# Cross-attention block on one core: score products in four 32-row tiles with unmasked keys, and every round as straight code

## The reference, cut to what matters

```python
def attention(q, k, v, mask):                      # A and B
    scores = jnp.einsum('bhqd,bhkd->bhqk', q, k) / jnp.sqrt(jnp.float32(HD))
    scores = scores * mask - 10000.0 * (1.0 - mask)
    probs = jax.nn.softmax(scores, axis=-1)
    return jnp.einsum('bhqk,bhkd->bhqd', probs, v)
...
scores = jnp.einsum('bhtd,bhsd->bhts', Q, K) * scale     # C
scores = jnp.where(mask, scores, jnp.float32(-jnp.inf))
attn = jax.nn.softmax(scores, axis=-1)
```

## Time and profile before

| what | value |
|---|---|
| median of 3 runs | 1069.2 us (1064.68 to 1073.83) |
| profiled execution, span | 1072.6 us, 3.4 us above the median |
| mean granted TensorE clock | 0.947 of full |
| PE, PEld busy | 967.9 us (90%), 929.0 us (87%) |
| DVE, ACT, POOL busy | 866.5 us (81%), 576.3 us (54%), 561.3 us (52%) |
| instructions | 23111, of them PE 8336 matmuls |
| chain that ended last | PE 44%, DVE 32%, issue 11%, POOL 6%, ACT 6% |
| DMA | 25.74 MB, 24 GB/s on average |

### The profile page before, as it was taken

One profiled execution on the slowest core, in us unless ns is written; L12 is line 12 of the kernel. 1 busy time (PEld: TensorE's weight loads), 2 busy tenths in 40 slices (PEclk: granted clock), 3 DMA queues, 4 the chain that ended last, 5 costly groups with the idle time before them and its releaser, 6 DMA issues.

```text
span 1072.6 us, 23111 instructions
## 1 busy us (share of the span) xinstructions
PE 967.9 (90%) x8336; PEld 929.0 (87%) x8336; DVE 866.5 (81%) x1946; ACT 576.3 (54%) x1109; POOL 561.3 (52%) x566
## 2 busy tenths in 40 slices
PE   6977799999999998999999898999999899998876
PEld 6866798989989998988999898998999899998875
DVE  6586979888897978889797988889797888778553
ACT  3444646565474556646464656547455664646342
POOL 2254647457283746638274745728474563727221
PEclk9589999998999899999989999899989999898995
DMA  5030100101000010101001010100101010000000
GB/s 192 0 96 1 36 1 12 37 11 36 11 10 26 9 35 10 35 10 35 10 0 35 10 35 10 35 10 0 35 10 35 10 36 1 26 13 7 17 10 10
DMA packets 32936, 25.74 MB, mean 24 GB/s; under 512 B 12672, under 2 KB 32000, under 8 KB 32896
## 3 DMA queue, kind: packets, MB, share of 16 engines
q1 hardware_dynamic: 32896, 25.20, 7.9%
HBM read 20.99 MB, written 4.19 MB: 23 GB/s over the span
## 4 chain that ended last, share of the span: by engine, by line
PE 44%; DVE 32%; issue 11%; POOL 6%; ACT 6%; DVEq 1%; DMA 0%; ACTq 0%; POOLq 0%; SPq 0%
PE s_bank L504 12%; PE pj L446 10%; PE s_bank L493 7%; PE pj L431 6%; DVE o L866 5%; PE pj L460 4%; DVE rmax_A L852 3%; POOL prob_AC L1089 2%; DVE prob_AC L847 2%; DVE stats L892 2%; DVE z_A L906 2%; PE pj L521 2%; DVE rmax_C L852 2%; PE s_bank L482 2%; DVE z_B L906 2%
## 5 line engine op out<-in xcount | busy, mean ns | idle before, releaser
L683 ACT ACTIVATE k<-pj,kbias,consts 128x256 f32<-128x256 f32 x192 | 92.7, 564 | 143.1 <-PE pj L431 143.1
L1065 POOL TENSOR_TENSOR veps<-mv,eps 128x2 f32<-128x2 f32 x64 | 15.6, 243 | 263.2 <-DVE mv L898 263.2
L1089 POOL TENSOR_TENSOR prob_AC<-prob_AC,rmax_C 128x512 f32<-128x512 f32 x64 | 65.6, 1054 | 125.4 <-DVE rmax_C L852 125.4
L692 ACT ACTIVATE prob_AC<-prob_AC 128x512 f32<-128x512 f32 x128 | 81.1, 636 | 89.5 <-POOL prob_AC L1089 89.4
L1096 POOL TENSOR_TENSOR h_lo<-g,h_hi 128x512 fp32r<-128x512 f32 x64 | 81.4, 1292 | 47.3 <-DVE h_hi L1051 47.3
L482 PE MATMUL s_bank<-k,q 64*128 64x128 f32 x1536 | 100.3, 281 | 6.3 <-ACT q L670 3.8
L482 PEld LDWEIGHTS s_bank<-k,q 64*128 64x128 f32 x1536 | 91.0, 191 | 14.2 <-issue 4.7
L504 PE MATMUL s_bank<-vz_C,prob_AC 128*128 128x66 f32 x512 | 74.7, 316 | 16.5 <-ACT prob_AC L698 16.5
L504 PEld LDWEIGHTS s_bank<-vz_C,prob_AC 128*128 128x128 f32 x512 | 72.7, 231 | 19.5 <-issue 19.4
L1080 POOL TENSOR_TENSOR prob_AC<-prob_AC,maskA_off 128x512 f32<-128x512 f32 x64 | 79.9, 1284 | 17.2 <-DVE prob_AC L847 17.2
L1080 POOL TENSOR_TENSOR prob_B<-prob_B,maskB_off 128x512 f32<-128x512 f32 x64 | 83.0, 1329 | 10.7 <-DVE prob_B L847 10.6
(11 more groups left out here) (199 smaller groups left out, 3324.7 us busy)
## 6 DMA issues: line engine op xcount, KB each, us to landing
x_in<-in_x SPq DMA_DIRECT2D x16, 256.0 KB, 2.7
ctx_b<-in_ctx SPq DMA_DIRECT2D x16, 256.0 KB, 2.9
ctx_c<-in_ctx SPq DMA_DIRECT2D x16, 256.0 KB, 2.8
out<-y SPq DMA_DIRECT2D x16, 256.0 KB, 2.2
g<-in_w_M SPq DMA_DIRECT2D x2, 1024.0 KB, 7.1
maskB<-in_mask_Bx1xSxS_ff SPq DMA_DIRECT2D x32, 64.0 KB, 2.6
prob_AC<-in_w_A_qkv SPq DMA_DIRECT2D x1, 768.0 KB, 4.5
prob_B<-in_w_B_kv SPq DMA_DIRECT2D x1, 512.0 KB, 6.1
```

What stands on the lines that cost most here:

```text
L683: last = nc.scalar.activation(k2[:, m, :, s, :], k_all[:, m], ACT.Identity, bias=kbias[:, "ABC".index(a), s, m:m + 1], scale=parity[:, 2 + ...
L692: nc.scalar.activation(p2, p2, ACT.Exp).then_inc(exped[a], 1)
L1089: nc.gpsimd.tensor_tensor(p3, p3, rmax[a][:, r, :].unsqueeze(2).broadcast_to([P, BL * TILE, S]), ALU.subtract).then_inc(shifted[a], 1)
```

## The change

The keys are kept once (k1, without the parity scaling or the second copy): two activations, with the plain bias. A score product contracts over 32 partitions, which are one head pair (two heads), and streams 64 columns. There are 32 products for an attention: for each t, c, b2 the four row groups r = 0..3, and row group r writes bank r. All four banks are waited for before the first product and handed over with the last (t, c, b2). A bank now holds one row group for both tiles, so the order of head pairs in prob, sums and o changes, and with it the access patterns of masks, offsets, values and normalisation. The stationary operand q2 is as before. kbias is dropped. `run` has no loop: all rounds are straight code.

```diff
-        k2 = sb("k2", [P, KC, UB, 2, S])
+        k1 = sb("k1", [P, KC, UB, S])
...
-        def of_tile(m, a, r):
-
-            t = r // HALVES
-            m = m[:, :, :] if a == "A" else m[:, t * TILE:(t + 1) * TILE, :]
-            return m.rearrange("p b k -> p (b k)").unsqueeze(1).broadcast_to([P, BL, TILE * S])
+        def by_tile(scores):
+
+            return scores.rearrange("p (t c) k -> p t c k", t=T)
+
+        def of_tiles(m, a):
+
+            if a == "A":
+                m = m.rearrange("p b k -> p (b k)").unsqueeze(1).broadcast_to([P, T, TILE * S])
+            else:
+                m = m.rearrange("p (t b) k -> p t (b k)", t=T)
+            return m.unsqueeze(2).broadcast_to([P, T, KC, TILE * S])
...
-            for i in range(first, min(FIRST, last + 1)):
-                body(i)
-            with eng.Fori(FIRST, U) as i:
-                body(i)
-            for i in range(U, last + 1):
+            for i in range(first, last + 1):
                 body(i)
...
+                wait_score_banks(f"S_{a}", i, R - 1)
                 for t in range(T):
-                    wait_score_banks(f"S_{a}", i, HALVES * (t + 1) - 1)
                     for c in range(KC):
                         for b2 in range(TILE):
-                            for half in range(HALVES):
-                                rows_ = slice(half * S, (half + 1) * S)
-                                bank = s_bank[t * HALVES + half][:, :].rearrange(
-                                    "p (c s b k) -> p c s b k", c=KC, s=2, b=TILE)
-                                mm = nc.tensor.matmul(bank[:, c, :, b2, :],
+                            for r in range(R):
+                                rows_ = slice(r * 2 * HD, (r + 1) * 2 * HD)
+                                at = ((t * KC + c) * TILE + b2) * S
+                                mm = nc.tensor.matmul(s_bank[r][:, at:at + S],
                                                       q2[rows_, c, t * TILE + b2].rearrange("p e q -> p (e q)"),
-                                                      k2[rows_, c, t * TILE + b2], start=True, stop=True)
-                                if (c, b2) == (KC - 1, TILE - 1):
+                                                      k1[rows_, c, t * TILE + b2], start=True, stop=True)
+                                if (t, c, b2) == (T - 1, KC - 1, TILE - 1):
                                     mm.then_inc(scored[a], 1)
...
-                for s in range(2):
-                    for m in range(KC):
-                        last = nc.scalar.activation(k2[:, m, :, s, :], k_all[:, m], ACT.Identity,
-                                                    bias=kbias[:, "ABC".index(a), s, m:m + 1],
-                                                    scale=parity[:, 2 + s:3 + s])
+                for m in range(KC):
+                    last = nc.scalar.activation(k1[:, m, :, :], k_all[:, m], ACT.Identity,
+                                                bias=bias[:, BK[a] + m:BK[a] + m + 1])
...
-                nc.vector.tensor_tensor(prob[a][:, r, :, :], s_bank[r][:, :].rearrange("p (n k) -> p n k", n=BL),
-                                        of_tile(m, a, r), f).then_inc(masked[a], 1)
+                nc.vector.tensor_tensor(by_tile(prob[a][:, r, :, :]),
+                                        s_bank[r][:, :].rearrange("p (t c k) -> p t c k", t=T, c=KC),
+                                        of_tiles(m[:, :, :], a), f).then_inc(masked[a], 1)
...
-                            o[rows_, t * TILE:(t + 1) * TILE, half * BL:(half + 1) * BL, :],
-                            sums[rows_, :, e * HD:(e + 1) * HD].rearrange("p (n b) f -> p b n f", b=TILE),
-                            rden[a][rows_, r, :].rearrange("p (n b) -> p b n", b=TILE).unsqueeze(3).broadcast_to(
-                                [S, TILE, BL, HD]), ALU.mult)
+                            o_r[rows_],
+                            sums[rows_, :, e * HD:(e + 1) * HD].rearrange("p (c b) f -> p c b f", c=KC),
+                            rden[a][rows_, r, :].rearrange("p (c b) -> p c b", c=KC).unsqueeze(3).broadcast_to(
+                                [S, KC, UB, HD]), ALU.mult)
...
-                    p3 = prob[a][:, r, :, :]
-                    nc.gpsimd.tensor_tensor(p3, p3, of_tile(maskA_off if a == "A" else maskB_off, a, r),
-                                            ALU.add).then_inc(offset[a], 1)
+                    p4 = by_tile(prob[a][:, r, :, :])
+                    m = maskA_off if a == "A" else maskB_off
+                    nc.gpsimd.tensor_tensor(p4, p4, of_tiles(m[:, :, :], a), ALU.add).then_inc(offset[a], 1)
```

More of the change, by code:

```diff
@@ L158, in build @@
         qbias = sb("qbias", [P, 2, 2, KC])
-        kbias = sb("kbias", [P, 3, 2, KC])
         brow = sb("brow", [P, 3, H])
@@ L501, in values @@
                 pe.wait_ge(turned_in[a], R * u + r + 1)
-                t, half = divmod(r, HALVES)
+                half, s = divmod(r, 2)
                 for n in range(BL):
-                    last = nc.tensor.matmul(s_bank[r][:, n * TILE * VW:(n + 1) * TILE * VW],
-                                            prob[a][:, r, n, :], vz[a][:, t, half * BL + n, :, :],
+                    t, c = divmod(n, KC)
+                    at = c * T + t
+                    last = nc.tensor.matmul(s_bank[r][:, at * TILE * VW:(at + 1) * TILE * VW],
+                                            prob[a][:, r, n, :], vz[a][:, t, half * BL + c * 2 + s, :, :],
                                             start=True, stop=True)
@@ L809, in finish_biases @@
                     if stage != "C":
[L810 to L814, removed]
+                        last = nc.vector.tensor_scalar(qbias[:, "AB".index(stage), e, :],
+                                                       bias[:, BQ[stage]:BQ[stage] + KC],
+                                                       qscale[:, e:e + 1], None, ALU.mult)
+                        if e == 1:
+                            last.then_inc(bias_done, 1)
+                    elif e == 1:
+                        nc.vector.nop().then_inc(bias_done, 1)
             def low_part(name, i, bias_cols=None):
@@ L858, in normalise @@
                     dve.wait_ge(summed[a], R * u + r + 1)
-                    t, half = divmod(r, HALVES)
+                    half, s = divmod(r, 2)
                     sums = s_bank[r][:, 0:BL * TILE * VW].rearrange("p (n v) -> p n v", v=VW)
+                    o_r = o[:, :, half * BL:(half + 1) * BL, :].rearrange("p b (c s) f -> p s c b f", s=2)[:, s]
                     nc.vector.reciprocal(rden[a][:, r, :], sums[:, :, 2 * HD]).then_inc(inverted[a], 1)
```

## The result

The changed kernel took 1094.85 us in the median (1093.48 to 1117.82, 4 runs) against 1069.22 (1064.68 to 1073.83, 4 runs). The ratio is 1.0206, 95% interval 1.0165 to 1.0247; a second measurement beside the experiments gave 1.0231 (1.0169 to 1.0294). The 1117.82 is an execution at a lower clock throughout (0.82 against 0.93 to 0.94), which the ratio leaves out, so the ratio is not the quotient of the medians. The change is slower by about 2%, or 22 us; the interval does not say on which side of 2% it lies. The forecast was 1075, range 1059 to 1092. The profiled execution has a span of 1091.7 us, 19.1 over that of before.

What follows compares the result with a forecast made beforehand. The prediction took a round to be TensorE work plus waits anchored on other engines; +10.5 - 1 - 2.2 + 0 - 1.9 = +5.4 on the 1069.2 us median gave 1074.6, forecast 1075, range 1059 to 1092.

Steps and rivals of the forecast that it cites:

- rival (d): Low clock in all rounds, from score bursts streaming half the columns and TensorE idling 0.75 us longer: 1088 us, chance 0.12.
- same: Outcome of a measured time within about 1% of no change, between 1058.5 and 1079.9 us; chance 0.53.
- start, filling, draining: Filling and draining rounds: four bursts waiting for q begin sooner through cheaper keys, 0.35 us each; taken as -1 us.
- Part 1: Score matmuls: the 128-column load sets the step, so four tiles keep the burst at 1.99 us.
- Rival (a): Score bursts: only two tiles run side by side or issue falls short; burst 3.98 us, about 1142 us, chance 0.13.
- Part 2: Score handover at C: first mask starts 0.75 us later, M.H0 waits longer, 14 rounds, +10.5 us.
- Part 3: Keys on ScalarE: 1.1 us less, 48 times; nothing sooner in steady rounds, -1 us in filling and draining rounds.
- Part 4: Straight code instead of the loop: 0.2 us less in each of 11 loop passes, -2.2 us.
- Part 5: Access shapes of mask products, offsets, row maxima and normalisation: same number and elements, taken as 0 us.
- the clock's term: 1.2 GHz stretches 25 to 32 us into every second round: one fewer through changed round length, -1.9 us.

Runs made afterwards that it cites:

- e1_straight: The kernel before with every round as straight code and nothing else changed; ratio 0.9989 to the kernel before.
- e3_wide: The changed kernel with each score product except a tile's last streaming 128 columns again; ratio 1.0091 to the kernel before.
- e9_half: The changed kernel with the second head's queries left out of the score products, so loads are 64 columns wide; ratio 1.0136 to the kernel before.
- e2_late: e1_straight plus the late handover alone: all four score banks waited for at the start and handed over at the end; ratio 1.0079 to the kernel before.
- e10_narrow: e1_straight with each score product streaming 64 columns instead of 128, half of the scores not computed; ratio 1.0006 to the kernel before.
- e11_warm: e1_straight with A.K's twelve matmuls done an extra time between transposes and value products of C; median 1063.54 us, ratio 0.9892 to the kernel before.
- e7_fill: e1_straight with A.K's twelve matmuls moved between the transposes and the value products of C; ratio 1.0004 to the kernel before.
- e5_vfirst: The changed kernel with VectorE's vz_B copies moved ahead of the four masks of C; ratio 1.0242 to the kernel before.

## Why the prediction was right, and where its sizes were off

The direction and the mechanism of the first two parts were right: no gain from four tiles, a loss from the handover. The size was 5 us where 22 were measured. That the time still falls into the range is narrow, and in part luck: the ratio puts it at 1091.2 us (1.0206 x 1069.2), 0.8 us below the upper bound, the median of 1094.85 us lies above it, the range reached that far only because it took in rival (d), and the outcome held most likely, with 0.53, was "same". The 19.1 us between the profiled executions divide so:

| where | predicted | measured | from |
|---|---|---|---|
| full-clock length of rounds 4 to 16: handover, with bursts, keys and shapes | +10.5 (14 rounds) | +10.3 | full-clock lengths: 12 x 61.3 + 59.9 = 795.5 in the changed kernel, 12 x 60.5 + 59.2 = 785.2 in e1_straight |
| straight code | -2.2 | -2.3 | e1_straight less before, 796.5 - 798.8 |
| low clock, rounds 4 to 16 | -1.9 | +6.0 | excess over full-clock lengths: 812.8 - 795.5 = 17.3, in e1_straight 796.5 - 785.2 = 11.3 |
| start, filling, draining | -1 | +5.1 | -3.9 to the start of round 2, +5.5 in rounds 2 and 3, +3.5 from round 17 |

**Part 1**, the burst: 1.99 forecast, 1.95 measured, and the reason (the load, not the stream or the issue) is shown by e3_wide and e9_half. Four matmuls stand together at the head of the burst, where before there were two:

```profile
543.71 0.34 PE L459 MATMUL s_bank<-k,q 32*128 32x64 f32 x4
```

Rival (a) is out. **Part 2**, the handover: the first mask moved by 0.75 us as worked out, M.H0's wait to 1.33 (forecast 1.2), and e2_late shows it alone, at 1.0 us a round: beside M.H0's wait (0.8 us more), the wait at C.AO grew by 0.2 (1.25 to 1.46 us), which the prediction had put at nothing, since it took the delay to be paid once. **Part 3**, the keys: 52 us of ScalarE saved, and no wait gone from a steady round. TensorE's waits for q ahead of the scores fell from 6.3 to 5.5 us in all (forecast 1), one of them at the scores of A in round 2, 1.33 to 0.89 us between starts. It was not isolated further. **Part 4**: right in size, two thirds of it by the shorter passes and the rest by the place of a stretch. **Part 5**, the shapes: the mask product takes 683 ns (685 before), the offset of B 1331 against 1329, normalisation 289.

**The step that failed is the clock's term.** It said that "the change alters neither" of the things ahead of a stretch, looked only at the one place where stretches stood, and took one fewer. The change did alter what stands ahead of another place, the scores of A and the wait for oT_lo: half the streamed columns. In place of -1.9 us the term measured +6.0. Rival (d), at 0.12, named this cause and gave 1088 with a stretch in all rounds; eleven of thirteen had one and the time was 1094.85. That a longer round would shift the stretches came true in e2_late, by far more than the one forecast (one stretch instead of six, 9 us less); with the narrow stream this gain was lost, and the stretches at the new place came on top. The other term that failed is the start, filling and draining, forecast at -1 us from the keys alone and measured at +5.1.

**What stays open.** The filling rounds 2 and 3 take 112 to 115 us in all seven kernels with four tiles and 128-column loads, wide stream or narrow, and 105 to 107 in the others and in e9_half. The clock there is lower (0.79 to 0.83 against 0.87 to 0.90): each of the seven has a stretch of 17.1 us at 1.2 GHz in these rounds, and none of the others has one over 6.8. TensorE's idle time in them is about equal (22 to 24 us, 20 to 27 in the others). That e9_half is among the others points at the width of the loads; no experiment says why. Why the clock falls at some of these waits in one round and not in the next, with the same instructions, is open too. The start up to round 2 varies by itself, 46.2 and 51.1 us in two executions of the changed kernel, so that line of the table is not to be read closely.

## What to carry to other kernels

Splitting a contraction over more row tiles gave nothing here, since it doubled the number of 128-column loads (1.99 and 1.95 us a burst); halving the load's columns took the burst to 1.09 us. Before splitting, look whether a burst is bound by its loads, and read what the wait behind the burst is anchored on: three bursts shorter by 0.9 us each did not shorten a full-clock round. When outputs move from "two banks halfway" to "all banks at the end", price the handover for whoever reads first. On a kernel that is 90% TensorE, count the rounds with a low-clock stretch before and after, and look at every place where TensorE waits, even for little over 1 us: the clock fell here in or behind waits at the value products (1.2 to 1.65 us) and at C.AO (1.3 to 2.5 us). A few repeated matmuls in such a wait can be worth more than removing it.

## What the runs showed of the hardware that was not expected

- A burst of 128 instructions (64 loads, 64 matmuls) on four row tiles ran in 1.09 us, 8.5 ns an instruction.
- With nothing but the stream width of three 2 us bursts changed, the clock fell behind them or did not: 64 columns in the changed kernel and e10_narrow, 128 in e3_wide and e1_straight. The loads and the duration of the bursts were the same.
- Idle entries of 1.19 to 1.65 us at the value products and of 1.3 to 2.5 us at C.AO, with transposes and fp32 products around them, stood at nearly all falls to 1.2 GHz in rounds 4 to 16 (the clock fell in them or within 2.7 us behind them); the same entries stood in rounds without a fall. Filling the one at the value products with twelve 256-column matmuls removed all six falls (e11_warm), and shifting the same matmuls there from behind moved the falls to the next wait (e7_fill).
- Removing M.H0's wait of 1.3 us in each round, which takes a full-clock round from 61.3 to 60.4 us, made the kernel no faster (e5_vfirst, 1.0242 against 1.0231), since the clock was low for 109 us of rounds 4 to 16 instead of 61.
